# Graph attention and routed experts on one core: node rows added to the attention's mean by the transfers that load them

## What is computed

```python
x = x + gnn0(layernorm(x), edges)      # graph attention, 8 heads of 64, softmax over incoming edges
x = x + ffn0(layernorm(x))             # 8 experts, each takes its top 256 nodes
x = x + gnn1(layernorm(x), edges)      # mean of neighbours, two products, silu
x = x + ffn1(layernorm(x))             # 64 experts, top 2 per node, and a shared one
```

## Time and profile before

| | |
|---|---|
| Time, median of 3 runs | 2376.68 us (2372.86 to 2383.5) |
| Time of the profiled execution | 2382.49 us |
| Its span, first to last instruction | 2380.7 us |
| Busy over the span | PE 83%, DVE 72%, ACT 43%, POOL 43% |
| `phase_attend` in the trace | about 764.9 to 836.7 us |
| DMA, mean over the span | 223 GB/s |

### The profile page before, as it was taken

The page is one execution under the profiler, slowest core; times in us unless marked ns, Lnnn a source line. Parts: engine busy times, 40 slices in busy tenths (PEclk is TensorE's granted clock), DMA queues, the critical chain, the costliest instruction groups (busy, mean ns, idle before and its releaser), DMA issues. The chain is left out here.

```text
span 2380.7 us, 35341 instructions
## 1 busy us (share of the span) xinstructions
PE 1980.9 (83%) x8428; PEld 1253.8 (53%) x8428; DVE 1708.6 (72%) x4081; ACT 1020.8 (43%) x3220; POOL 1025.6 (43%) x1051
## 2 busy tenths in 40 slices
PE   5957888888887625259999999898898999999996
PEld 4735666666665323124433444354345777777753
DVE  6647888988888762376666666477755888899956
ACT  2325777777786602465566665345000111111110
POOL 1037777777772404247777777400001111111134
PEclk9978999999999657779999999999999999999998
DMA  5648887888883734677777777785314889999956
GB/s 148 125 157 244 241 245 236 243 239 245 242 238 94 290 108 94 169 265 224 223 224 224 224 224 224 233 307 194 111 32 133 300 301 327 337 344 337 365 188 229
DMA packets 272786, 531.38 MB, mean 223 GB/s; under 512 B 43123, under 2 KB 121563, under 8 KB 272403
## 3 DMA queue, kind: packets, MB, share of 16 engines
q0 software_dynamic: 80544, 261.97, 37.9%
q1 hardware_dynamic: 173587, 234.36, 29.5%
q10 hardware_dynamic: 18464, 32.84, 4.2%
HBM read 446.42 MB, written 83.42 MB: 223 GB/s over the span
## 5 line engine op out<-in xcount | busy, mean ns | idle before, releaser
L851 POOL DMA_INDIRECT g_G<-tab,src_of_item x440 | 443.6, 1008 | 178.7 <-issue 108.5
L916 PE MATMUL g_psA<-g_G,g_oh 128*128 128x261 f32 x1760 | 443.0, 398 | 60.3 <-DVE g_G L1066 47.5
L1221 PE MATMUL g_psA<-g_G,g_oh 128*128 x832 | 386.1, 607 | 77.0 <-SPq L1177 70.0
L1161 POOL DMA_INDIRECT g_G<-tab,src_of_tile x392 | 370.8, 946 | 164.5 <-issue 80.1
L973 ACT ACTIVATE g_G<-g_G 128x64 f32<-128x64 f32 x1760 | 425.1, 336 | 0.0
L1264 DVE TENSOR_TENSOR acc<-acc,g_psA 128x512 f32 x416 | 285.8, 687 | 184.9 <-PE g_psA L1221 143.9
L916 PEld LDWEIGHTS g_psA<-g_G,g_oh 128*128 128x128 f32 x1760 | 326.9, 194 | 122.9 <-DVE g_G L1066 59.8
L2660 DVE STREAM_TRANSPOSE mo_xT<-mo_g 32x128 f32<-32x128 f32 x1152 | 348.0, 302 | 15.0 <-issue 0.3
L1221 PEld LDWEIGHTS g_psA<-g_G,g_oh 128*128 128x128 f32 x832 | 146.1, 190 | 294.8 <-issue 293.8
L2450 PEld LDWEIGHTS mo_bank<-mo_xT,mo_w 128*128 128x128 f32 x2304 | 267.3, 193 | 57.8 <-DVE mo_xT L2660 38.4
L2354 POOL DMA_INDIRECT mo_g<-tab,mo_slot x72 | 68.0, 945 | 512.2 <-DVE mo_xT L2660 383.4
(11 more groups left out here) (422 smaller groups left out, 2388.8 us busy)
## 6 DMA issues: line engine op xcount, KB each, us to landing
mo_w<-in_L_ffn_w SPq DMA_DIRECT2D x216, 512.0 KB, 6.4
ys<-mo_y ACTq DMA_DIRECT2D x72, 256.0 KB, 5.5
g_ot<-reld SPq DMA_DIRECT2D x27, 512.0 KB, 5.8
ys<-sg_zeros SPq DMA_DIRECT2D x24, 512.0 KB, 4.4
g_G<-tab,src_of_item POOLq DMA_INDIRECT x440
g_pen<-pend SPq DMA_DIRECT2D x216, 32.0 KB
tab<-fi_row SPq DMA_DIRECT2D x25, 261.0 KB, 2.5
xmid<-at_x SPq DMA_DIRECT2D x25, 256.0 KB, 5.1
```

The lines of the kernel that those rows point to most:

```text
L851: q.indirect_dma_start(G[:, j % RING, :], None, tab0, bass.IndirectOffsetOnAxis(K.src[:, j:j + 1], 0)).then_inc(gs[g % 3], 16)
L916: ins = tens.matmul(psA[u][:, f, 0:HW], oh[:, n % OR, h, :], G[:, r + h, f * HW:(f + 1) * HW], start=(h == 0), stop=(h == SUP - 1))
L1161: g.indirect_dma_start(G[:, (j + 1) % MR, :], None, table, bass.IndirectOffsetOnAxis(K.src1[:, j:j + 1], 0)).then_inc(got[j % MR], 16)
L1221: tens.matmul(psA[n % MB][:], oh[:, n % MO, :], G[:, ds(tile1 % MR, 1), :].rearrange("p o d -> p (o d)"), start=True, stop=True).then_inc( ...
```

## The change

The input's tile is no longer loaded first and added by POOL. DVE writes the mean directly into `x1[:, n, :]`; when it has, POOL issues a transfer that reads the tile of x from DRAM and adds it to what stands in `x1` (`accum_op=ALU.add`). `xl[n]` now says that the tile is complete, and SP's store and DVE's `stats(n)` wait for it. The ring `mean`, the semaphore `summed`, SP's 25 loads and the clearing of the last tile are gone. `stats` and `finish` run TB = 4 steps behind `mean_of` and not 2. The `xl` semaphores are taken by `gather_sem`, which keeps them allocated.

```diff
-        mean = p.sb("mean", [P, TB, D])
-        summed = p.sem("summed")
-        xl = [p.sem(f"xl{n}") for n in range(NT)]
+        xl = [p.gather_sem(f"xl{n}") for n in range(NT)]
 # SP
-            for n in range(NT):
-                if last(n):
-                    s.wait_ge(epsd, 1)
-                s.dma_start(x1[0:rows_of(n), n, :], tile_rows(a["x"], n)).then_inc(xl[n], 16)
             for n in range(NT + NB):
                 if n < NT:
-                    s.wait_ge(summed, n + 1)
+                    s.wait_ge(xl[n], 16)
                     s.dma_start(xmid[n * P:(n + 1) * P, :], x1[:, n, :]).then_inc(sx, 16)
 # POOL
             for n in range(NT):
-                g.wait_ge(xl[n], 16)
                 g.wait_ge(meaned, n + 1)
-                nc.gpsimd.tensor_tensor(x1[:, n, :], x1[:, n, :], mean[:, n % TB, :], ALU.add).then_inc(summed, 1)
+                g.dma_start(x1[0:rows_of(n), n, :], tile_rows(a["x"], n), accum_op=ALU.add).then_inc(xl[n], 16)
 # DVE
-            vv.memset(x1[:, NT - 1, :], 0.0)
             def mean_of(n):
-                wait(v, summed, n - TB + 1)
-                vv.tensor_tensor(mean[:, n % TB, :].rearrange("p (h d) -> p h d", h=H0),
+                vv.tensor_tensor(x1[:, n, :].rearrange("p (h d) -> p h d", h=H0),
             def stats(n):
-                v.wait_ge(summed, n + 1)
+                v.wait_ge(xl[n], 16)
-            for n in range(NT + 3):
+            for n in range(NT + TB + 1):
...
-                if 0 <= n - 2 < NT:
-                    stats(n - 2)
+                if 0 <= n - TB < NT:
+                    stats(n - TB)
                 for j, e in enumerate(ends):
-                    if n == e + 2:
+                    if n == e + TB:
                         finish(j)
```

## The result

| | before | after |
|---|---|---|
| Median of 9 runs | 2379.74 us (2372.86 to 2388.55) | 2391.59 us (2385.42 to 2395.33) |
| Ratio to before | | 1.0039, 95% interval 1.0024 to 1.0054 |
| Span of the profiled execution | 2380.7 us | 2387.8 us |
| `phase_attend`: DVE's first instruction in it to its first in the next | 71.9 us | 77.4 us |

By the ratio of the runs the change costs 0.39%, 9.3 us, where 9.5 were predicted. The interval reaches from 5.7 to 12.9 us, and the two medians lie 11.9 us apart, so the agreement to 0.2 us is closer than the measurement can tell. The cost is clear of zero; its ratio is within the 0.5% called "no change that can be told", though the interval passes it a little.

What follows compares the result with a forecast made beforehand. DVE bounds phase_attend to about 816 us, then ACT; after the change the DMA engines do. Last norming 769.8 + 73.5 - 4.1 = 839.2 instead of 829.7, so 2376.7 + 9.5 = 2386 us, range 2371 to 2401.

Steps and rivals of the forecast that it cites:

- The bound moves to the DMA engines: In phase_attend the DMA engines, with 20 us to spare before, are full from the first tiles on; phase 9.5 us longer.
- An adding load costs 1.6 us, between 1.46 and 2.04: DMA engines' work per 256 KB adding load in phase_attend, taken from adding scatters; a plain transfer takes 0.69 us.
- The rival with 2.04: Each adding load in phase_attend costs the DMA engines 2.04 us, as the scatters did: +20 us, 2397 us; chance 0.22.
- Full engines read 1.0: The DMA share in phase_attend was to stand near 1 from about 771 to 835 us.
- The term of 73.5 us: All DMA work of phase_attend: 24.4 adding loads at 1.6 us plus 50 stores at 0.69 us, 22 us more than before.
- Six stores, 4.1 us, are left when ACT norms the last tile: End of phase_attend: up to six stores of normed rows needn't be done by then, so 4.1 us come off the sum.
- Start: Start of phase_attend: first load lands at 772.7, 2.4 us later; about +1 us by the first group of four.
- DVE's relief of 6.8 us vanishes in waits: In phase_attend DVE's 25 means get 6.8 us shorter without POOL's additions, but waits take up the gain.
- POOL's issue, 1.0 to 1.6 us: POOL's time to issue each adding load in phase_attend; at most 1.88 us per tile, 47 us in all, beside other work.
- Rival 2: Adding into SBUF costs the DMA engines only 0.7 us, ACT bounds, phase_attend ends 4 us earlier, 2373 us; chance 0.15.
- Rival 3: Four steps between mean and statistics are too few if loads land after 9.4 us: +2 us, 2379 us; chance 0.08.
- No difference outside the phase: Only phase_attend changes; the prediction saw no cause for a difference elsewhere in the kernel.

Runs made afterwards that it cites:

- ten places: The changed kernel with ten places for normed tiles instead of six, SP's order kept: phase 76.5 us, last norming at 68.3 us.
- the mixed kernel: The kernel before with tiles 5, 7, ... 23 added by their transfers, the other fifteen by POOL: ratios 1.0018 and 1.0014.

## Why the prediction was right, and where it wasn't

- *The bound moves to the DMA engines:* right, shown by the 25 stores more (5 us before, 14 after) and by the share of 1.09 to 1.10. Without the addition the last norming came 14.5 to 15.2 us earlier.
- *An adding load costs 1.6 us, between 1.46 and 2.04:* the measured 1.46 is the low end. The rival with 2.04 falls. Whether the scatters' 2.04 held restarts, as argued, or was the price of scattering into DRAM, no run separates. Work in all 71.8 us, not 73.5.
- *Full engines read 1.0:* wrong. With adding loads and stores together they read 1.09 to 1.10, so that 71.8 us of work pass in about 66. The term of 73.5 us was 7.5 us too long, 1.7 by the cost of a load and 5.8 by this. A part of it could be read before: the earlier trace rows have a full stretch at 1.05. The rest comes with the adding loads and not with the second queue: with plain loads on POOL's queue beside SP's stores the share is 1.04 from 777 to 797 us, at 386 GB/s.
- *Six stores, 4.1 us, are left when ACT norms the last tile:* wrong. The engines' share from 837 to 838 is 0.00; only the last store was left, 0.7 us:

```profile
837.00:838.00 1.00, 0.00 (x0) 0.00 (x0) 0.14 (x1) 0.82 (x2) 0.00 (x0) 1.00 0.00 0
```

  The prediction had the engines full up to the last norming, and here its reasoning failed. The adding loads were over by about 825 us (392 GB/s from 825 to 829, a rate of plain transfers alone), ACT waited for a store for the last time before 824.63, and then the stores caught up with ACT: the share is 1.03 from 829 to 833 and 0.66 from 833 to 837. With ten places ACT did leave some 4 us of stores behind it. The prediction took 3.4 us too much off its sum here. The idle engines from 833 on add 1 to 2 us. Put together, 769.8 + 66 - 0.7 and 1 to 2 us of idling make 836 to 837, and 837.18 was measured; the prediction said 839.2. The start of the DMA work was right: the share is 0.09 from 769 to 770 us and 1.07 from 770 to 771. The near hit of the total rests in part on the two errors' opposite signs, and its last part on luck: by the phase of the profiles the change costs 5.5 us in the first pair and 11.4 in the second, and the forecast was 9.5.
- *Start:* the first statistics at 772.13 (predicted 772.7), the first group of four normed from 783.98, 1.4 us later than before (predicted about 1).
- *DVE's relief of 6.8 us vanishes in waits:* right, 7.2 us: DVE's wait for ACT's root grew from 11.3 to 20.9 us, and 5.8 us for loads are new.
- *POOL's issue, 1.0 to 1.6 us:* median 0.85 us, below the range, mean 1.0. It isn't on the path.
- *Rival 2, adding is free:* falls with the plain loads, which gained what it said and more. The rule of the Trainium skill ("DMA: Bandwidth & Descriptors", Anatomy of one DMA) is 2.0 us and bytes over 436 GB/s, by which 256 KB move in 0.60 us. The plain load's 0.78 us of work lies near that, the adding one's 1.46 doesn't.
- *Rival 3, a lead of four is too short:* landings were 8.0 us (up to 9.5), near the 8.8 where it would decide, but a longer lead made it worse. Falls.
- *No difference outside the phase:* there may be one. From the end of the phase to the end of the span it took 1543.8 and 1540.8 us in the two profiles of before and 1545.2 and 1546.9 in those of after. The cause stays open.
- *The median, 2386 us:* 2391.59 was measured. 3.1 of the 5.6 us are the kernel before, whose median of nine runs is 2379.74 and not the 2376.7 of three.

## What to carry to other kernels

A transfer that adds cost the DMA engines here about twice a plain one of the same bytes (1.46 against 0.72 to 0.78 us). It can pay only where an engine is the bound and the DMA engines have more than that to spare over the whole stage, not only at its end; no run here shows a case where it did pay, the mixed kernel with its spare DMA time included. When transfers share the engines, a sum of work is a first bound; then look at which transfer somebody waits for, since a queue with many loads in flight can delay the stores of another, as with the lead of eight. Moving work off POOL frees DVE only where no other POOL addition fills the place beside DVE's: in the mixed kernel ten fewer additions left the sum of DVE's means at 23.8 us.

## What the runs showed of the hardware

- 256 KB with addition into SBUF, direct from POOL: 1.46 us of the engines, 0.85 us of issue (median); plain from POOL: 0.78 and 0.54; stores from SP: 0.72. The adding loads moved the same 6.40 MB in 3536 packets where the plain ones took 1968.
- The DMA share of full engines read 1.09 to 1.10 with adding loads and stores together. It read 1.05 with plain transfers on one queue, and 1.04 with plain transfers on both.
- The two-input mean on DVE took 683 ns beside POOL's issues of transfers and 1062 ns beside its additions.
- From the last norming to the next phase it took 5.5 us at a granted PE clock of 1.00 (2.4 GHz), 7.3 us at a mean clock of 0.64 and 7.4 at 0.62, and 8.1 us at 0.50 (1.2 GHz, ten places).
- Twenty-five plain loads at the pace of the work, on POOL's queue, were better than the same loads issued at once ahead of the stores in SP's: last norming 57.5 against 60.9 us, with POOL free of additions in both.
